# Queries and keys held on chip through gating, forget-gate math in two groups, half of the expert weights prepared during routing

## The reference, cut to what matters

```python
x = x + mlstm(q=layernorm(x), k=ctx, v=ctx)      # gates: concat(q, k, v) @ (256*3, 8) + bias, twice
    log_fg = log_sigmoid(fgate); cs = cumsum(log_fg)
    log_D = tril(cs[i] - cs[j] + igate[j]); D = exp(log_D - rowmax)
    C = (q @ k.T / sqrt(32)) * D
    h = C / (max(|rowsum C|, exp(-rowmax)) + 1e-6) @ v ; per-head layernorm * weight
x = x + moe(layernorm(x))                        # scores (8), top 2, softmax over the two
    y = sum_k p_k * ((silu(x @ w1_e) * (x @ w2_e)) @ w3_e)
```

## Time and profile before

| | us |
|---|---|
| median of three runs | 681.81 |
| the profiled execution: device time | 680.75 |
| its span | 679.0 |
| gating (to the last gate matmul) | 0 to 62.0 |
| gate math and the fill of mixing (to the first key-value product) | 62.0 to 88.4 |
| mixing and its tail | 88.4 to 272 |
| routing to the first expert matmul | 272 to 316 |
| experts | 316 to 679 |

### The profile page before, as it was taken

How to read it: one execution, slowest core, us unless ns; L and a number is a source line. 1 busy time by engine, 2 the same in 40 slices (tenths; PEclk the granted TensorE clock), 3 DMA queues, 4 the chain that set the end, 5 groups by cost and what they waited for, 6 DMA issues and landing times.

```text
span 679.0 us, 15003 instructions
## 1 busy us (share of the span) xinstructions
PE 565.5 (83%) x3608; PEld 465.6 (69%) x3609; DVE 465.2 (69%) x976; ACT 331.7 (49%) x736; POOL 305.3 (45%) x312
## 2 busy tenths in 40 slices
PE   3876098988988985124999999999999999999993
PEld 1332077877877864012888888888888888888883
DVE  3664336788878887993676767667677767676763
ACT  3444345566666753001555555555555555555551
POOL 2233325465655742002354545455555555454532
PEclk9999588999999995555999999999999999999998
DMA  9885575566666633601133333323333333333332
GB/s 284 251 297 187 173 203 159 175 210 209 200 202 220 192 113 110 255 4 44 33 56 56 50 60 48 62 47 63 47 59 52 55 55 54 55 52 58 48 47 24
DMA packets 72293, 77.51 MB, mean 114 GB/s; under 512 B 12930, under 2 KB 64266, under 8 KB 72268
## 3 DMA queue, kind: packets, MB, share of 16 engines
q0 software_dynamic: 15712, 25.73, 20.5%
q1 hardware_dynamic: 47564, 42.59, 20.4%
q10 hardware_dynamic: 8992, 8.92, 3.8%
HBM read 53.99 MB, written 23.21 MB: 114 GB/s over the span
## 4 chain that ended last, share of the span: by engine, by line
issue 42%; DVE 16%; POOL 12%; DMA 11%; PE 11%; SPq 4%; ACT 2%; DVEq 0%; ACTq 0%; POOLq 0%
POOL xg L1093 8%; DMA out_rows<-ys,index 6%; PE bank L1208 5%; POOL out_rows L1102 4%; DMA qT_scratch<-qt 4%; PE dots L1190 3%; DVE c L799 3%; DVE ohn L942 2%; DVE ohp L941 2%; DVE st L704 1%; DVE tot L838 1%; DVE mu L833 1%; DVE wden L834 1%; DMA gv<-in_gkv 1%; DVE mv L708 1%
## 5 line engine op out<-in xcount | busy, mean ns | idle before, releaser
L1102 POOL DMA_INDIRECT out_rows<-ys,index x71 | 112.9, 1590 | 155.7 <-DVE ys L994 149.3
L1000 DVE TENSOR_TENSOR w3l<-w,w3h 128x1024 fp32r<-128x1024 f32 x71 | 87.1, 1227 | 30.9 <-issue 29.9
L1093 POOL DMA_INDIRECT xg<-token_table,index x71 | 70.4, 991 | 74.7 <-DVE index L959 52.9
L671 ACT CAST w3h<-w 128x1024 fp32r x71 | 74.4, 1048 | 20.1 <-issue 20.1
L1208 PE MATMUL bank<-aug,c 128*128 128x99 f32 (+2 forms) x512 | 65.2, 282 | 15.5 <-DVE c L799 15.3
L1322 PE MATMUL bank<-w3l,hth 128*128 128x256 f32 x284 | 76.5, 302 | 1.7 <-DVE w3l L1000 1.7
L1208 PEld LDWEIGHTS bank<-aug,c 128*128 128x128 f32 x512 | 61.2, 196 | 22.4 <-DVE c L799 19.9
L1323 PE MATMUL bank<-w3h,hth 128*128 128x256 f32 x284 | 70.8, 282 | 0.0
L977 DVE TENSOR_TENSOR htl<-bank,hth 128x512 fp32r<-128x512 f32 x71 | 49.1, 691 | 25.2 <-ACT hth L661 25.2
L994 DVE TENSOR_SCALAR ys<-bank,pc 128x256 f32<-128x256 f32 x71 | 34.4, 484 | 46.5 <-PE bank L1326 46.5
L1294 PE MATMUL weighs<-w12l,xh 128*128 x144 | 62.2, 432 | 1.1 <-DVE xl L966 1.1
(11 more groups left out here) (169 smaller groups left out, 1221.6 us busy)
## 6 DMA issues: line engine op xcount, KB each, us to landing
x<-in_x SPq DMA_DIRECT2D x32, 256.0 KB, 3.3
wst<-in_w12T POOLq DMA_DIRECT2D x26, 256.0 KB, 3.7
aug<-in_ctxv SPq DMA_DIRECT2D x16, 264.0 KB, 3.6
ct<-in_ctxT SPq DMA_DIRECT2D x16, 256.0 KB, 4.8
qT_scratch<-qt SPq DMA_DIRECT2D x16, 256.0 KB, 3.7
kt<-in_ctxT SPq DMA_DIRECT2D x16, 256.0 KB
qbd<-qT_scratch SPq DMA_DIRECT2D x64, 64.0 KB
out_rows<-x ACTq DMA_DIRECT2D x16, 256.0 KB, 2.2
```

The lines of the kernel that those rows point to most:

```text
L671: nc.scalar.copy(W3H[i][:], w3[:, bass.ds(e, 1)].rearrange("p a k d -> p (a k d)")).then_inc(w3h_ready, 1)
L1000: v.tensor_tensor(W3L[i][:], w3[:, bass.ds(e, 1)].rearrange("p a k d -> p (a k d)"), W3H[i][:].bitcast(F32), ALU.subtract).then_inc(w3l_re ...
L1093: q.indirect_dma_start(out=XG[x][:], out_offset=None, in_=table, in_offset=bass.IndirectOffsetOnAxis(ap=index[:, j:j + 1], axis=0)).then_i ...
L1102: q.indirect_dma_start(out=out, out_offset=bass.IndirectOffsetOnAxis(ap=index[:, j:j + 1], axis=0), in_=YS[o][:], in_offset=None, compute_ ...
```

## The change

The pieces 16 to 31 of `w12h` and `w12l` become the home of the transposed queries and the transposed context of the 16 batches until mixing has used them: `kept(flat_h, b)` and `kept(flat_l, b)`. The scratch for queries and for gate values, the tiles `KT`, `QTB`, `QT1`, `CT1` and their loads and stores go; `QBD` is filled from `kept` on chip. Mixing prepares piece b + 16 in step b, when batch b is done with. Nothing of `w12` is prepared in gating or gate math: pieces 0 to 15 are loaded, rounded and subtracted after mixing, ahead of `w3` on SP, ahead of the one exponential on ACT, ahead of the gathers on POOL; PE waits for all 32 before its first expert tile.

The gate values go straight from `GS1` to `gi`, `gf` by two DMAs per batch. The gate math runs once for the 32 rows of batches 0 to 3 inside gating and once for the 96 rows of batches 4 to 15 inside mixing steps 0 to 3. The memsets of `QBD` and `KVB` go from DVE after gating to POOL at the start. The gating loops, and PE's mixing loop, are unrolled.

```diff
+LEAD = 4
+AHEAD = slice(P - LEAD * NH, P)
+REST = slice(0, P - LEAD * NH)
+KEPT = PIECES - B
...
+        def kept(flat_, b):
+            return flat_[:, bass.ds((b + KEPT) * HID, HID)].bitcast(F32).rearrange("p (k s) -> p k s", k=NK)
...
 SP, gating and on to the first step of mixing
-            gating(sp, stage1, peeled=8)
+            for b in range(B + 5):
+                old = b - 5
...
+                if 0 <= old:
+                    sp.wait_ge(gates_ready, old + 1)
+                    at = (old - LEAD) % B * NH
+                    for k, dst in enumerate((gi, gf)):
+                        sp.dma_start(dst[at:at + NH, :], GS1[old % 2][k * NH:(k + 1) * NH, :]
+                                     ).then_inc(gate_out[old % 2], 16)
+                if b == B:
+                    pair_rows(0)
+                    sp.wait_ge(zeroed, 1)
+                    load_queries(0, 0)
+                if b == B + 1:
+                    sp.wait_ge(parts_out, 16 * (1 + PARTS))
+                    load_gates(0, 0)
...
+                if isinstance(b, int) and b == LEAD - 1:
+                    pair_rows(1)
+                    sp.wait_ge(parts_out, 32 * (1 + PARTS))
...
+            for n in range(KEPT):
+                sp.dma_start(room(flat_l, n, HID), w12T[:, n * HID:(n + 1) * HID]).then_inc(late_in[n], 16)
-            sp.wait_ge(w_lo, W2 + B)
+            sp.wait_ge(w_lo, W2)
...
 ACT, gating; then the ends of mixing steps 0 and 1; then routing
+                if b == 8:
+                    act.wait_ge(late_consts, 16 * N_LATE)
+                    forget(0)
+                if b == 11:
+                    gate_parts(0, 0, 2)
+                    decays(0)
+                if b == 12:
+                    gate_parts(0, 2, 3)
...
+                if isinstance(b, int) and b == 0:
+                    forget(1)
+                if isinstance(b, int) and b == 1:
+                    gate_parts(1, 0, 2)
+                    decays(1)
+                    gate_parts(1, 2, 3)
...
+            for n in range(KEPT):
+                high(n, room(flat_l, n, HID), 16, late_in[n])
...
 DVE, gating; then mixing
+            for b in range(B + 1):
+                stage1(b, b % 4)
+                if b == 8:
+                    preactivation(0)
+                if b == 10:
+                    maxima(0)
+                if b == 11:
+                    three_parts(dve, v, negM, AHEAD, m_parts, 0)
+                if b == 14:
+                    columns(0, bank[4])
...
+                    if c == 1 and isinstance(b, int) and b == 1:
+                        preactivation(1)
+                        maxima(1)
...
+                if isinstance(b, int) and b == 2:
+                    columns(1, bank[7])
...
+                if isinstance(b, int) and b == 1:
+                    three_parts(dve, v, negM, REST, m_parts, 2 * PARTS - 1)
...
 POOL
-                    load_w(b + B, i, W2 - 1 + b)
+                    load_w(b + KEPT, i, b - 1)
-                    low(b - 1 + B, wst[o][:], W2 + b)
+                    low(b - 1 + KEPT, wst[o][:], b)
+                if isinstance(b, int) and b == 1:
+                    gate_rests(1)
...
+            for n in range(KEPT):
+                low(n, room(flat_l, n, HID), W2 + n + 1)
...
 PE
+                if b == 13:
+                    columns(0, bank[4])
...
+            pe.wait_ge(qT_ready, B)
             exponents(0, 0, 0)
-            mixing(pe, step)
+            pe.wait_ge(gates_ready, B)
+            for b in range(B + 3):
+                step(b, b % 2)
...
             pe.wait_ge(tables, 1)
+            pe.wait_ge(w_lo, PIECES)
```

More of the change, by code:

```diff
@@ L438, in _, with pair_rows @@
-            sp.wait_ge(zero_out, 64)
-            sp.wait_ge(cols_ready, 1)
+            def pair_rows(part):
+                rows_ = (AHEAD, REST)[part]
+                lo, hi = ((0, LEAD), (LEAD, B))[part]
+                for q in range(PARTS):
+                    sp.wait_ge(g_parts, PARTS * part + q + 1)
+                    sp.dma_start(g_dram[lo:hi, q], parts[rows_, 1, q, :]).then_inc(parts_out, 16)
+                sp.wait_ge(m_parts, (2 * PARTS - 1) * (part + 1))
+                sp.dma_start(negM_dram[:, lo * NH:hi * NH, :].rearrange("q a s -> a q s"), parts[rows_, 0]
+                             ).then_inc(parts_out, 16)
@@ new lines, in gate_parts, with decays @@
+            def gate_parts(part, lo, hi):
+                rows_ = (AHEAD, REST)[part]
+                for q in range(lo, hi):
+                    act.wait_ge(g_rest, PARTS * part + q + 1)
+                    src = g[rows_, :] if q == 0 else rest[rows_, 1, q - 1, :]
+                    nc.scalar.copy(parts[rows_, 1, q, :], src).then_inc(g_parts, 1)
+            def decays(part):
+                rows_ = (AHEAD, REST)[part]
+                act.wait_ge(g_ready, part + 1)
+                act.wait_ge(dcol_zero, 1)
+                nc.scalar.activation(dcol[rows_, 0, :], g[rows_, 0:P], ACT.Exp, bias=negM[rows_, P - 1:P])
+                nc.scalar.activation(dcol[rows_, 1, :], negM[rows_, P:S], ACT.Exp, bias=M[rows_, P - 1:P])
+                nc.scalar.activation(dcol[rows_, 2:4, :].rearrange("p a s -> p (a s)"), mx[rows_, :], ACT.Exp,
+                                     scale=-1.0).then_inc(dcol_ready, 1)
@@ L558, in _ @@
-            act.wait_ge(pair_in, 32)
-            nc.scalar.activation(fa[:], gf[:], ACT.Abs, bias=fb[:, 0:1]).then_inc(abs_ready, 1)
-            act.wait_ge(abs_ready, 1)
-            nc.scalar.activation(fe[:], fa[:], ACT.Exp, scale=-1.0).then_inc(pair_act, 1)
-            act.wait_ge(pair_act, 1)
-            nc.scalar.activation(fl[:], fe[:], ACT.Ln, bias=1.0).then_inc(log_ready, 1)
-            for q in range(PARTS):
-                act.wait_ge(g_rest, q + 1)
-                src = g[:] if q == 0 else rest[:, 1, q - 1, :]
-                nc.scalar.copy(parts[:, 1, q, :], src).then_inc(g_parts, 1)
@@ L1232, in step @@
                     ins.then_inc(x2t_psum, 1)
+                if isinstance(b, int) and b == 2:
+                    pe.wait_ge(o1_taken, 2)
+                    columns(1, bank[7])
                 if main:
```

329 lines of the change are left out of this document (139 added, 190 removed).

## The result

| | us |
|---|---|
| kernel after, median of 20 runs | 683.41 (680.30 to 685.71) |
| kernel before, median of 20 runs beside them | 680.34 (678.13 to 685.04) |
| ratio | 1.0046 [1.0028, 1.0063] |
| the profiled execution's span, after (before: 679.0) | 680.9 |

What follows compares the result with a forecast made beforehand. It took gating to fill no engine, PE (91%) to bound mixing and DVE routing. Terms -15.8 + 4.5 + 17 = +5.7 on 680.75 gave 686.45; with 1.06 for the median, 687.5 us, range 680 to 692.

Steps and rivals of the forecast that it cites:

- the decisive term: Routing: DVE's 37 us and 20.5 us of POOL subtractions add up, +17 us, bounds 0 and 20.5.
- no contention in routing: Rival: one-hot tiles slip between POOL's subtractions, routing costs 0 to 3 us, total 672; chance 0.22.
- by the rule alone the full 20.5: Routing: if DVE and POOL exclude each other for their whole length, the term is 20.5 us instead of 17.
- gating and fill: From the start to batch 0's first key-value product: from 88.43 to about 72.6, -15.8 us.
- the second group: Gate math in mixing steps 0 to 3: DVE 2.6 and about 1.9 more, +4.5 us, bounds 0 and 13.5.
- from 20.5 I take off 2 us: Routing: 2 us off for DVE's PSUM reads, reductions and own waits, plus 16 x 0.1 for overlapping starts, giving +17.
- The wait in the middle: Gating, first group of gate math: PE idles 5.7 us for a tile behind ACT's logarithms and DVE's normalization.
- The slow batch behind it: Gating: after PE's idle time the next batch runs at 1.2 GHz, 2.2 us more plus 0.7, together 2.9.
- gating hides its gate math: Rival: DVE runs ahead, PE's wait stays short, 6 to 11.8 us come back, total 679; chance 0.17.
- `three_parts` and ACT's queue make 1.9 more: Mixing, second group: step 2's ACT work queues behind split and exponentials; with `three_parts`, about 1.9 us beyond DVE's delay.
- The third rival: ACT's queue in mixing step 1 holds up step 2, PE falls to 1.2 GHz, total 696.5 us; chance 0.17.
- 0 for the rest of mixing: Mixing after the second group: fewer loads, POOL still subtracts 16 pieces, pace stays 10.36 us; 0, bounded at 3.

Runs made afterwards that it cites:

- the other executions of the same program: Changed kernel with no subtractions in routing (667.03 us), routing's subtractions on DVE (679.36), no subtractions in mixing (665.93), or all subtractions on DVE (665.10).
- the two other executions of the same program: Changed kernel without POOL's 16 subtractions in routing (667.03 us), and changed kernel with those 16 subtractions on DVE (679.36 us).
- the study's two best versions: Changed kernel, gate math later, values early: all subtractions on DVE (654.08 us); or eight pieces prepared on POOL in gating, other subtractions on DVE (658.36 us).
- the fastest kernel: Changed kernel with all subtractions on DVE, first group of gate math later, batch 0's values and keys loaded early: 654.08 us, ratio 0.963.

## Why the prediction was right or wrong

**The direction and the main mechanism held, the size did not.** The forecast was +5.7 us for the profiled execution; it came out at +1.9, and the medians at +3.1. "Within 1%" was the likeliest class by 0.39 to 0.38 for "slower", so that it came true says little. The mechanism of the decisive term, POOL's subtractions stopping DVE's operations in routing, is shown by the kernel that leaves them out (routing -14.4 us, the exact difference) and by the row-by-row match of one operation per subtraction. The first rival, "no contention in routing", is refuted. The rule of the Trainium skill (SBUF — State Buffer, "Who interferes with whom") that the forecast weighed is borne out for these tiles. The same section says that on this chip a `tensor_reduce` never contends with GpSimd, nor does an instruction with at most one input in SBUF outside the two-port modes; the 0.42 us rows beside the subtractions agree. So "by the rule alone the full 20.5" left out the section's own exceptions.

**The step that failed is the sum's largest term, routing: too large by 2.6 us.** Its size is the same in every execution. The misses in gating and fill (-2.8) and in the second group (+2.1) are about as large in this profile, pull against each other, and change by 2 to 3.5 us between executions of the same program.

- *Routing, 17 forecast, 14.4 measured.* The step was "from 20.5 I take off 2 us" for reductions, reads of matmul results and DVE's waits for itself, and 1.6 for overlapping starts. The subtractions took 20.1 us. In the first 5.5 of them (to 271.5) DVE's list is 2.1 us longer than in the kernel without subtractions (5.5 us against 3.4 for the same operations, `slotS` to `sloti`), so 3.4 came off there. In the other 14.6 it lost 12.4, and 2.2 is the operations' own time. Together 5.6 came off where I had taken 3.6.
- *Gating and fill, -15.8 forecast, -18.6 measured, and -16.4 to -18.6 with the other executions of the same program.* Of the start I took 1.7 us between 0.5 and 3.3; it is 3.0 (20.38 to 17.40), which is also what 0.75 MB take at 264 GB/s, not 3.3. PE needs 2.42 us per batch and not 2.5. The wait in the middle was longer than reckoned, 6.72 against 5.7: I had not seen that the gate copy ahead of ACT's logarithms waits for a store. The slow batch behind it cost 1.3 and not 2.9, since the granted clock was back by 39 us. That was a short one: in the other four executions this batch took 4.57 us, 2.2 more than a normal one. The other pieces cost 2.2 together, against 3.2. The last gate matmul ended at 61.1, not 64.9 (in the others 61.7 to 63.3); the fill from there took 8.8 us instead of 7.7, of which my own terms had given only 7.2 (67.5 + 3.6 + 0.4 + 0.6 is 72.1, and 72.6 was written). The rival "gating hides its gate math" is refuted as it stood: the 6.72 us are there. But moving `preactivation` two steps takes most of the wait away, so the cost was mainly the place in the list and not the work.
- *The second group, 4.5 forecast, 6.6 measured, and 4.0 to 7.5 with the two other executions of the same program.* The step was "`three_parts` and ACT's queue make 1.9 more". DVE's part before the product was right: 2.6 forecast, a wait of 2.55. Of the rest I had put nothing on the clock, and it is part of it: the mean granted clock is 0.86 here and 0.79 and 0.76 in the two others, against 0.88 before. The second wait, 4.75 us in this execution, is DVE's and not ACT's: the 0.17 us operation `wabs` stands 4.37 us. It follows `columns`, for which I had no cost in mixing; that this delay is what put it behind POOL's chain is my reading of the order, and no kernel moved `columns` alone. Nor is `wabs` the cost of the stretch by itself: with 1.45, 2.38 and 1.21 us of it the stretch was 35.4, 38.9 and 37.5. How the cost divides between that hold and the clock stays open. The third rival (ACT's queue in front of step 2) is refuted as to its wait, since PE's wait names DVE's `c` and `c` stands behind `wabs` in DVE's list; its fall to 1.2 GHz did come.
- *Experts, 0 forecast, -1.1.* That is within the 363.5 to 365.4 us of all kernels. PE was granted 2.4 GHz about 5 us after the first transpose of gathered rows (322.4), in the kernel before about 8 (322.3). I have no cause for it and tried none.

It was luck that batch 3's product stands at 107.9 where 108.5 was forecast: the two stretches before it were off by -2.8 and +2.1.

**What the prediction did not see at all** changed no term of it, and was worth more than the change. The earlier trace rows made me ask what POOL's subtraction does to DVE in routing. I did not ask what the sixteen subtractions in mixing were doing already, since the change leaves their number alone ("0 for the rest of mixing", which the pace of 10.43 against 10.36 confirms). The answer was in the profile of before: `wden`, 16 columns, 1446 ns at the mean. Taking the subtractions away takes it to 204 ns, as it freed the tiles in routing, and the study's two best versions are built on it. Freeing it in the old kernel alone gives 2.2%.

**Where the gain of the change went.** 18.6 us from gating and fill were bought with 14.4 in routing, where the displaced preparation meets an engine that is full, and 6.6 in mixing's first steps, where in part PE itself ran at the lower clock. With POOL's subtractions moved to DVE in both kernels (in the old one those of mixing, in the changed one all), the exchange is still even (663.97 and 665.1). Only with the first group of gate math placed later and the values loaded early does it pay: 654.08, about 10 us below the old kernel with the same cure. Those two ratios, 0.963 [0.959, 0.967] and 0.978 [0.973, 0.984], don't overlap.

## What to carry to other kernels

In a profile, look for tiny operations with a long mean: a DVE operation on 16 columns at 1.4 us is a wait that no wait column shows, and the instruction of POOL that ends with it is its price. "POOL is idle there" is no cover for moved work when DVE is the bound and both read tiles in on-chip memory: 20 us of POOL cost 14 us of DVE, and the same work on DVE 9.6 us. And when a change moves work from one part to another, price the part that receives it by its fullest engine, and ask of each late insertion what its wait does to PE's clock and which short DVE operation it puts beside POOL's chain. Where two kernels differ by 2 us in one stretch, look at a second execution of the same program first.

## What the runs showed of the hardware

- In routing one DVE operation got through per POOL operation (twelve rows of 1.19 to 1.31 us, three of them above; POOL's mean 1.29). In mixing's step 2 it did not: `wabs` stood through POOL operations back to back, 4.37 and 3.14 us. Which of the two gets its turn between POOL instructions is open; the rows tell only that both happen.
- `wden` began at 184.22, 0.35 us before the row of the subtraction with which it ended, and beside POOL's DMA issue. With the same issue and no subtraction behind it, its mean is 204 ns, so the issue alone doesn't hold it. Either it comes to its tiles later than its row begins, or POOL's instruction earlier; that is open too.
- The same wait of PE was followed by either clock. In gating 2.20 us were followed by 1.67 us for four gate matmuls, at a granted clock of 0.50, and 2.18 us of the fastest kernel by 1.04, at 1.00. In step 1 of mixing 2.55 us were followed by a values group of 1.97 us in the changed kernel, and 2.56 us by one of 3.62 in the kernel without subtractions in routing. What decides between them is open. After 6.72 us the transposes took 1.12 us instead of 0.66.
